# Attention scores issued three units ahead of the transposes, and the ternary weights made during V's projection

## The reference

```
q, k, v = x Wq^T, x Wk^T, x Wv^T          # 16 heads of 64, per batch
q = q * min(cond_1, 4)
attn = softmax(causal(q k^T / 8))
y = (attn v) Wo^T
scale = max(|y| over the row) / 127;  q_y = clip(round(y / scale), -128, 127) * scale
alpha = mean(|weight|);               q_w = clip(round(weight / alpha), -1, 1) * alpha
out = x + q_y q_w^T + bias
```

## Time and profile before

| | us |
|---|---|
| median of 3 runs (lowest, highest) | 2136.11 (2134.82, 2138.73) |
| the profiled execution | 2134.82 |
| its span from first to last instruction | 2132.7 |

### The profile page before, as it was taken

How to read it: one execution, slowest core, us unless ns; L and a number is a source line. 1 busy time by engine, 2 the same in 40 slices (tenths; PEclk the granted TensorE clock), 3 DMA queues, 4 the chain that set the end, 5 groups by cost and what they waited for, 6 DMA issues and landing times.

```text
span 2132.7 us, 33722 instructions
## 1 busy us (share of the span) xinstructions
PE 2009.8 (94%) x10062; PEld 1609.4 (75%) x10062; DVE 1421.7 (67%) x3282; ACT 1119.8 (53%) x2504; POOL 908.7 (43%) x823
## 2 busy tenths in 40 slices
PE   6999998999999999999999999998898999999998
PEld 5788886787787787777877877777676777777776
DVE  7656555777778777778777777678876645454554
ACT  5444444767677677677677677676666100000000
POOL 4433332444445445435435435343533544444442
PEclk9999999999999999999999999999999999999999
DMA  5755443433443433443433443553444332333322
GB/s 158 247 178 167 161 146 119 143 113 98 143 153 102 141 113 108 135 151 109 139 108 112 139 143 116 185 154 120 141 131 119 114 118 89 118 98 108 109 97 79
DMA packets 199667, 278.42 MB, mean 131 GB/s; under 512 B 11040, under 2 KB 146208, under 8 KB 198560
## 3 DMA queue, kind: packets, MB, share of 16 engines
q1 hardware_dynamic: 199584, 277.40, 40.8%
HBM read 176.69 MB, written 67.11 MB: 114 GB/s over the span
## 4 chain that ended last, share of the span: by engine, by line
PE 48%; issue 23%; POOL 15%; DVE 9%; DMA 2%; ACT 2%; POOLq 0%; SPq 0%; DVEq 0%; ACTq 0%
POOL prob L273 10%; PE proj_ps L548 8%; PE proj_ps L175 8%; PE s_ps L548 8%; PE t_ps L868 7%; POOL parts L365 5%; PE o_ps L619 5%; PE o_ps L868 5%; PE o_ps L317 2%; PE t_ps L283 2%; DVE prob L254 1%; DVE k_st L224 1%; DVE q_st L220 1%; DMA v_scratch<-v_out 1%; PE s_ps L243 1%
## 5 line engine op out<-in xcount | busy, mean ns | idle before, releaser
L175 PE MATMUL proj_ps<-parts 128*128 128x512 f32 x3072 | 841.6, 408 | 0.0
L273 POOL TENSOR_TENSOR prob<-prob,row_inv 128x128 f32<-128x128 f32 (+3 forms) x512 | 371.8, 726 | 743.2 <-DVE row_inv L267 743.1
L175 PEld LDWEIGHTS proj_ps<-parts 128*128 128x128 f32 x3072 | 545.7, 192 | 89.0
L261 ACT ACTIVATE prob<-prob,row_min 128x128 f32<-128x128 f32 (+3 forms) x512 | 287.4, 561 | 181.3 <-DVE row_min L254 178.6
L283 PE MATMUL t_ps<-ident,prob 128*128 128x128 f32 x1280 | 237.3, 284 | 80.2 <-POOL prob L273 78.6
L297 ACT ACTIVATE pt_hi<-t_ps 128x128 fp32r<-128x128 f32 (+3 forms) x512 | 220.9, 431 | 129.5 <-PE t_ps L283 126.0
L254 DVE CUSTOM_DVE_ANT_0 prob<-s_ps,mask 128x128 f32<-128x128 f32 (+3 forms) x512 | 249.8, 488 | 55.2 <-PE s_ps L243 25.3
L304 DVE TENSOR_TENSOR pt_lo<-t_ps,pt_hi 128x128 fp32r<-128x128 f32 (+3 forms) x512 | 248.7, 486 | 48.7 <-ACT pt_hi L297 47.6
L283 PEld LDWEIGHTS t_ps<-ident,prob 128*128 128x128 f32 x1280 | 147.6, 141 | 147.1 <-POOL prob L273 121.7
L604 ACT ACTIVATE yt_q<-t_ps 128x1024 bf16<-128x1024 bf16 x32 | 32.8, 1024 | 426.6 <-PE t_ps L597 426.6
L365 POOL TENSOR_TENSOR parts<-x_raw,parts 128x512 fp32r<-128x512 f32 x128 | 209.7, 1639 | 16.4 <-ACT parts L359 16.1
(11 more groups left out here) (108 smaller groups left out, 2903.5 us busy)
## 6 DMA issues: line engine op xcount, KB each, us to landing
x_raw<-xT SPq DMA_DIRECT2D x128, 512.0 KB, 5.5
...
v_st<-v_scratch SPq DMA_DIRECT2D x128, 256.0 KB, 2.8
k_sw<-k_st SPq DMA_DIRECT2D x128, 256.0 KB, 3.7
...
oT_scratch<-o_sum SPq DMA_DIRECT2D x64, 256.0 KB, 2.1
...
```

The source lines that it names most:

```text
L175: mm = pe.matmul(out, l, r, start=(k == 0 and i == 0), stop=(k == KT - 1 and i == 2))
L261: act.activation(prob[:, u % 4, 0:w], prob[:, u % 4, 0:w], ACT.Exp, bias=row_min[:, u % 4:u % 4 + 1], scale=-1.0, accum_out=row_sum[:, u % ...
L273: pool.tensor_tensor(prob[:, u % 4, 0:w], prob[:, u % 4, 0:w], row_inv[:, u % 4:u % 4 + 1].broadcast_to([P, w]), ALU.mult).then_inc(norm_d ...
```

## The change

1. **Order of a step.** S, M, E, I and N of a unit come one unit earlier against T, H and L: PE's list begins with S(6), T(3) and no longer with S(5), T(3), so that S runs three units ahead of T and not two. The projections are regrouped between them. S(8), which stood after J(0, 6), stands after J(0, 3); S(0), which stood after J(2, 6), stands after J(2, 5). T(10), which stood ahead of J(1, 7), stands behind it, while V(1) stays behind H(10) on ACT and behind L(10) on DVE. Odd x_low pieces on POOL follow N(2) to N(4).
2. **Ternary weights** move into V's projection: |weight| at the ends of pairs 2 to 5, the sum on PE after the first product of pair 6, rounding at the ends of pairs 6 to 13. The slices use the memory of x, are stored to `wf_scratch` and loaded again ahead of `load_o` in the last step with projections. The last group's middle steps become a loop.
3. **Start of V**: the x of pair 0 comes in two halves, the first ahead of all weights; the first weight slice is issued by ACT. In pairs 0 and 1 the splits of `wv_sums`, `ws_low` (all four now on DVE, two of them were on POOL), x and `v_out` are reordered: `v_high(0, q)` and `v_low(0, q)` come last.
4. **First step**: `load_x(0, 0)` is issued after pair 14's stores (it was after pair 1's). The wait for V's stores stands only ahead of `load_v`, and `swap_k` stands ahead of the first two `load_v`.

The core of the diff (the lists of ACT and DVE shift in the same manner as PE's):

```diff
+        def load_xv_first(sp, i):
+
+            for j in range(2):
+                sp.dma_start(xv_quad(0, i, j).rearrange("p (k s) -> p k s", s=P),
+                             xT[0, :, i * CH:(i + 1) * CH, 2 * j * P:(2 * j + 1) * P]).then_inc(xv_first_in[i], 16)
...
+        wf_tmp = [x_raw_all[:, i * D:(i + 1) * D] for i in range(2)]
+        wf_out = [x_raw_all[:, 2 * D + i * D // 2:2 * D + (i + 1) * D // 2].bitcast(BF16) for i in range(2)]
+        WF_ABS_FROM, WF_FROM = 2, 6
+
+        def load_wf(sp, n):
+            if n >= 2:
+                sp.wait_ge(*((wf_abs_done, n - 1) if n < KT + 2 else (wf_q_done, n - 1 - KT)))
+            sp.dma_start(wf_tmp[n % 2], wf[:, n % KT, :]).then_inc(wf_in[n % 2], 16)
+
+        def wf_abs(act, k):
+            act.wait_ge(wf_in[k % 2], (k // 2 + 1) * 16)
+            act.activation(wf_tmp[k % 2], wf_tmp[k % 2], ACT.Abs, accum_out=wf_sums[:, k:k + 1])\
+               .then_inc(wf_abs_done, 1)
+
+        def wf_add_partitions(pe):
+            pe.wait_ge(wf_abs_done, KT)
+            pe.wait_ge(v_lo_done, 4)
+            pe.matmul(wf_totals, ones[:, :], wf_sums[:, :], start=True, stop=True).then_inc(wf_total, 1)
+
...
+        def wf_ternary(dve, k):
+            raw = wf_tmp[k % 2]
+            dve.wait_ge(wf_in[k % 2], ((KT + k) // 2 + 1) * 16)
+            if k >= 2:
+                dve.wait_ge(wf_stored[k % 2], k // 2 * 16)
+            dve.tensor_scalar(raw, raw, alpha[:, 1:2], MAGIC, ALU.mult, ALU.add).then_inc(wf_chain, 1)
+            dve.wait_ge(wf_chain, 4 + 2 * k)
+            dve.tensor_scalar(raw, raw, MAGIC, 1.0, ALU.subtract, ALU.min).then_inc(wf_chain, 1)
+            dve.wait_ge(wf_chain, 5 + 2 * k)
+            dve.tensor_scalar(wf_out[k % 2], raw, -1.0, None, ALU.max).then_inc(wf_q_done, 1)
+
+        def store_wf(sp, k):
+            sp.wait_ge(wf_q_done, k + 1)
+            sp.dma_start(wf_scr[:, k, :], wf_out[k % 2]).then_inc(wf_stored[k % 2], 16)
+
+        def load_wf_q(sp):
+            sp.wait_ge(wqk_lo_done, 4 * NG)
+            sp.dma_start(wf_q, wf_scr).then_inc(wf_q_in, 16)
...
         def v_sp(sp):
-            load_wv(sp, 0)
-            load_xv(sp, 0)
-            for i in range(1, len(V_PIECES)):
+            load_xv_first(sp, 0)
+            load_wv(sp, 1)
+            load_xv_first(sp, 1)
+            for i in range(2, len(V_PIECES)):
                 load_wv(sp, i)
             load_xv(sp, 1)
             sp.dma_start(cond_bc[:, :], cond.rearrange("b a -> a b").broadcast_to([P, B])).then_inc(cond_in, 16)
@@ -937,15 +954,28 @@
                 if n == 1:
                     for c in (S4, S2, S1, S3):
                         sp.wait_ge(ws_lo_done[c], 1)
+                    load_wf(sp, 0)
+                    load_wf(sp, 1)
                     load_w(sp, 0)
+                if WF_ABS_FROM <= n < WF_ABS_FROM + KT // 2:
+                    for k in range(2):
+                        load_wf(sp, 2 * (n - WF_ABS_FROM) + 2 + k)
+                if WF_FROM <= n < WF_FROM + KT:
+                    k = n - WF_FROM
+                    store_wf(sp, k)
+                    if k + 2 < KT:
+                        load_wf(sp, KT + k + 2)
+                if n == WF_FROM + KT:
+                    for slot in wf_stored:
+                        sp.wait_ge(slot, KT // 2 * 16)
                     load_x(sp, 0, 0)
-            for slot in v_stored:
-                sp.wait_ge(slot, PAIRS * 2 * 16)
 
         def v_pe(pe):
             v_plain(pe)
             for n in range(1, PAIRS):
                 v_product(pe, n, A11)
+                if n == WF_FROM:
+                    wf_add_partitions(pe)
...
         def v_act(act):
+            load_wv(act, 0)
             for i, (k0, k1) in enumerate(V_PIECES):
-                act.wait_ge(wv_in[i], 16 * (k1 - k0))
                 if i == 0:
                     xv_split_plain(act, 0, 0, False)
+                    xv_split_plain(act, 0, 1, False)
                 if i == 2:
                     xv_split_plain(act, 1, 0, False)
                     xv_split_plain(act, 1, 1, False)
+                act.wait_ge(wv_in[i], 16 * (k1 - k0))
                 for k in range(k0, k1):
                     wv_split(act, k, False)
-                if i == 0:
-                    xv_split_plain(act, 0, 1, False)
             xv_split(act, 1, B11, False)
             xv_split(act, 1, B22, False)
             xv_split(act, 1, B21, False)
             ws_high(act, S4)
             ws_high(act, S2)
             ws_high(act, S1)
-            for q in range(2):
-                v_high(act, 0, q)
-            ws_high(act, S3)
             xv_split(act, 1, T2, False)
             xv_split(act, 1, T1, False)
+            ws_high(act, S3)
             xv_split(act, 1, T3, False)
             xv_split(act, 1, T4, False)
-            for q in range(2, 4):
+            for q in range(4):
                 v_high(act, 0, q)
...
         def v_dve(dve):
             for i, (k0, k1) in enumerate(V_PIECES):
                 if i == 0:
                     xv_split_plain(dve, 0, 0, True)
+                    xv_split_plain(dve, 0, 1, True)
                 if i == 2:
                     xv_split_plain(dve, 1, 0, True)
                     xv_split_plain(dve, 1, 1, True)
                 for k in range(k0, k1):
                     wv_split(dve, k, True)
-                if i == 0:
-                    xv_split_plain(dve, 0, 1, True)
-            wv_sums(dve)
             xv_split(dve, 1, B11, True)
             xv_split(dve, 1, B22, True)
             xv_split(dve, 1, B21, True)
+            wv_sums(dve)
             ws_low(dve, S4)
+            ws_low(dve, S2)
+            xv_split(dve, 1, T2, True)
             ws_low(dve, S1)
-            for q in range(2):
-                v_low(dve, 0, q)
-            xv_split(dve, 1, T2, True)
             xv_split(dve, 1, T1, True)
+            ws_low(dve, S3)
             xv_split(dve, 1, T3, True)
             xv_split(dve, 1, T4, True)
-            for q in range(2, 4):
+            for q in range(4):
                 v_low(dve, 0, q)
...
+                if n == WF_FROM:
+                    wf_scale(dve)
+                if WF_FROM <= n < WF_FROM + KT:
+                    wf_ternary(dve, n - WF_FROM)
 
         def v_pool(pool):
             xv_sums(pool, 1)
-            ws_low(pool, S2)
-            ws_low(pool, S3)
...
             def S(u):
-                if u >= 5 and old:
+                if u >= 6 and old:
                     scores(pe, o, u)
-                elif u < 5 and now:
+                elif u < 6 and now:
                     scores(pe, n, u)
...
-            J(0, 0)
-            S(5)
+            S(6)
             T(3)
-            J(0, 1)
-            J(0, 2)
+            J(0, 0, 1)
             YY(0)
-            S(6)
+            S(7)
             T(4)
-            J(0, 3)
+            J(0, 2, 3)
             YY(1)
-            S(7)
+            S(8)
             T(5)
-            J(0, 4)
+            J(0, 4, 5)
             PV(0)
-            J(0, 5)
             J(0, 6)
-            S(8)
+            S(9)
             T(6)
             J(0, 7)
+            J(1, 0)
             YY(2)
-            J(1, 0)
-            S(9)
+            S(10)
             T(7)
-            J(1, 1)
-            J(1, 2)
+            J(1, 1, 2, 3)
             YY(3)
-            S(10)
+            S(11)
             T(8)
-            J(1, 3)
-            J(1, 4)
-            S(11)
+            J(1, 4, 5)
+            S(12)
             T(9)
             YY(4)
             PV(1)
-            J(1, 5)
-            J(1, 6)
-            S(12)
+            J(1, 6, 7)
+            S(13)
             T(10)
-            J(1, 7)
+            J(2, 0, 1)
             YY(5)
-            J(2, 0)
-            S(13)
+            S(14)
             T(11)
-            J(2, 1)
-            J(2, 2)
+            J(2, 2, 3)
             YY(6)
-            S(14)
+            S(15)
             T(12)
-            J(2, 3)
-            J(2, 4)
-            S(15)
+            J(2, 4, 5)
+            if not old:
+                pe.wait_ge(v_sum_done, 4 * (PAIRS - 1))
+            S(0)
             T(13)
             YY(7)
             PV(2)
-            J(2, 5)
             J(2, 6)
-            if wf_part == 2:
-                wf_add_partitions(pe, n)
-            if not old:
-                pe.wait_ge(v_sum_done, 4 * (PAIRS - 1))
-            S(0)
+            S(1)
             T(14)
             J(2, 7)
             J(3, 0)
             Y(1, 0, 0, 1, 2)
-            S(1)
+            S(2)
             T(15)
-            J(3, 1)
-            J(3, 2)
-            Y(1, 0, 3, 4, 5)
-            S(2)
+            J(3, 1, 2)
+            Y(1, 0, 3, 4)
+            S(3)
             T(0)
-            J(3, 3)
-            J(3, 4)
-            Y(1, 0, 6, 7)
-            S(3)
+            J(3, 3, 4)
+            Y(1, 0, 5, 6, 7)
+            S(4)
             T(1)
             PV(3)
-            J(3, 5)
```

(33 more changed lines are left out.)

207 lines of the change are left out of this document (77 added, 130 removed).

## The result

The changed kernel takes 2242.93 us (median, 2235.26 to 2243.83) against 2135.73 us (2134.82 to 2138.73) of before: a ratio of 1.049, 95% interval 1.047 to 1.052, so 107 us slower. Its profiled execution took 2243.83 us with a span of 2241.8 us. The sign was forecast, and the time lies 37 us above the forecast and 3 us above the upper end of the range.

What follows compares the result with a forecast made beforehand. PE bound, nearly always busy, waiting on the latency from S(u) to N(u). Terms -78 - 3 + 82 + 42 + 30 - 8 + 2 + 4.5 = +71.5 on 2132.7 give 2204, plus 2.1 around the span 2206 us; range 2155 to 2240.

Steps and rivals of the forecast that it cites:

- The sign: Whole kernel: slower than before, chance 0.86; faster 0.12, within about 4 us 0.02.
- T's waits for POOL: PE's transposes T(u) waiting for POOL's N(u), 78.6 us before: all but about 1 us goes, -78.
- S(8), with T(4) on the way: PE at S(8) waits 2.65 us for the swap of k in each of 31 steps: +82; T(4) not named.
- S(0): PE at S(0) waits 1.36 us for its swap of k in 31 steps: +42, bounds 0.9 to 1.6 us a step.
- clock: PE's clock falls after S(8)'s gap in six steps of ten, 1.6 us each: +30; falls after T's waits go: -3.
- first step: First step: S(0) comes 6.8 us earlier and half of the clock's loss is saved: -8, bounds -2 and -10.
- start of V, sum of weights: V's projection: S1 ends later, +2; PE waits in pair 6 for the ternary weights' sum, clock probably falls, +4.5 once.
- Nothing of V(3) moves: Turn before S(8): V(3) stays first in ACT's and DVE's lists, starting on ACT 0.42 us after J(3, 7) ends.
- The prediction's own bound for this, 2.9 us: Upper bound of S(8)'s wait, if V(3) is late behind x_high on ACT, which had 0.26 us of room.
- Landing: Second DMA of the swap of k: lands 3.7 us after its issue, 3.5 at least.
- The gap at S(0) costs no clock: PE at S(0): a gap of 1.36 us is under 1.95 us, so the clock does not fall.
- x is through by then: First step: loads of x are done when the swap's second DMA goes at 349.3, so it lands near 353.4.

Runs made afterwards that it cites:

- The last kernel: Kernel with k projected ahead of q and the turn reordered (2065.6 us), with the first step's swap of k issued ahead of four loads of x: 2056.3 us.

## Why the prediction was wrong by 37 us

Measured terms, against the 71.5 us of the sum and 109 between the spans:

| term | predicted | measured |
|---|---|---|
| T's waits for POOL | -78 | -76 |
| S(8), with T(4) on the way | +82 | +110 (46 at T(4), 64 at S(8)) |
| S(0) | +42 | +44 |
| clock | +30 - 3 | +36 (22 falls more x 1.63) |
| first step | -8 | -3 |
| start of V, sum of weights | +2, +4.5 | +6 |
| PE's own work in a step | 0 | -11 (31 x 0.37) |

The measured terms sum to 106 of the 109 us. The forecast missed by less than its terms did: PE's shorter work, which it did not weigh, hid 11 us of the error.

- **S(8), the term that failed.** The chain of V(3), its swap and S(8) was right in every link but the first: "Nothing of V(3) moves", with 0.42 us from J(3, 7) to ACT. The place in the list doesn't move, but what stands ahead of it comes late. From the last matmul of J(2, 7) to the last of J(3, 7) PE took 10.30 us before and takes 9.16 now (medians of 30 steps), while ACT takes from V(2) to V(3) 10.47 and 10.38 us. Of the 1.14 us that PE is faster, 0.68 are idle time of T that is gone; the rest is PE's shorter work. So PE gets to J(3, 7) while ACT has two splits (1.16 us) left. That is 1.05 us in this step and 28 us in all. The prediction's own bound for this, 2.9 us, came from 0.26 us of idle time read in the slower kernel. The kernel with the splits behind V(3) shows it: 0.42 us and 2.66 us.
- **Where PE waits.** A part of the sum, 1.53 us, shows at T(4), which the prediction did not name. It changes nothing in the total: with H(2) ahead it goes to S(8).
- **S(0)**: 1.38 us where 1.36 was forecast; of the 0.86 us behind H(10) the kernel with V(1) ahead gives 0.8 back.
- **Landing.** The median of the landing of the swap's second DMA is 3.7 us after the change too, and the least 3.7 (before 3.5). The Trainium skill ("DMA: Bandwidth & Descriptors", section "Anatomy of one DMA") would give 2.6 us by its fit, which is for DMAs that GpSimd issues; the swap is SyncE's, and the trace has 1.1 us more.
- **Clock.** Falls behind 22 of 31 S(8) and not six in ten, at 43.89 - 42.26 = 1.6 us each, the predicted price. "The gap at S(0) costs no clock" failed once, where that gap was 2.65 us. The forecast reckoned with one gap of 2.65 us, and there are two, of 1.53 and 1.97 us; that the count came near six in ten is thus in part luck.
- **First step.** "x is through by then" was wrong: the swap, issued behind four loads of x, landed 7.6 us after its issue. The prediction had this inside its bounds of -2 to -10, near the wrong end. The last kernel shows the cause: with x behind the swap it lands in 3.8 us.
- **Start of V** and the weights: the end of V comes 6.0 us later, 6.5 were forecast. S1 starts 3.5 us later (66.12 us after 62.65), +2 was forecast; PE waits 2.7 us for the sum, 3.4 forecast. The clock did not fall there in this trace, but did in eight of the twelve experiments. How the 6.0 us divide is not shown, since the end of V varies by 3 us among equal lists. Rounding and the load of x(0, 0) are hidden, as forecast.
- **PE's work**: a step without a fall has 37.35 us of it after 37.7. The regrouped list costs PE less, and no run isolates why; nothing in the prediction weighed this.

The upper end of the range had room for 0.5 us more of waits a step, if the clock fell in all steps; the late V(3) took twice that in a plain step (1.05 us).
